# Splitting dt*u*B between the GpSimd and tensor engines by phase, and C of pair 0 on the vector engine in phases 7 and 11

## The reference, cut to what matters

```python
# d = 512 channels, 16 states per channel, 4 sequences (batches) of 512 steps
u = silu(conv1d(in_proj_w @ ctx) + conv_b)
dt_lo, Bm, Cm = split(x_proj_w @ u)              # 16, 16 and 16 rows
delta = softplus(dt_proj_w @ dt_lo + dt_proj_b)
def step(state, xs):                             # state: channels x 16
    dA = exp(d_t[..., None] * A)
    state = state * dA + (d_t * u_t)[..., None] * B_t[:, None, :]
    y_t = einsum('ben,bn->be', state, C_t)
y = (scan of step + D * u) * silu(layernorm(x))
x = x + tanh(g_xattn) * y
x = x + tanh(g_ffn) * ffn(layernorm(x))          # router, top 2 of 32 experts of rank 16
```

## Time and profile before

| | |
|---|---|
| median of 3 runs | 546.57 us |
| the three runs | 546.57, 546.42, 549.73 us |
| time of the profiled execution | 550.42 us |
| its span (first to last instruction) | 548.6 us |
| busy: PE, PEld | 490.2 us (89%), 361.4 us (66%) |
| busy: DVE, ACT, POOL | 481.8 us (88%), 393.8 us (72%), 456.5 us (83%) |
| mean granted PE clock | 0.96 |

### The profile page before, as it was taken

How to read it: one execution, slowest core, us unless ns; L and a number is a source line. 1 busy time by engine, 2 the same in 40 slices (tenths; PEclk the granted TensorE clock), 3 DMA queues, 4 the chain that set the end, 5 groups by cost and what they waited for, 6 DMA issues and landing times.

```text
span 548.6 us, 9113 instructions
## 1 busy us (share of the span) xinstructions
PE 490.2 (89%) x2962; PEld 361.4 (66%) x2962; DVE 481.8 (88%) x884; ACT 393.8 (72%) x704; POOL 456.5 (83%) x337
## 2 busy tenths in 40 slices
PE   6687989898888799999998999998999999899688
PEld 2156979767766486766776776657666666675654
DVE  3868999978989999979999999889899889999852
ACT  3268697847685878586886868595988888888542
POOL 0169999969999998979999999979799899887910
PEclk9656999999989899999999999999999999999799
DMA  5794000107520000047230000068100000000001
GB/s 102 265 340 158 1 2 1 39 7 268 193 76 2 2 1 32 27 154 254 78 97 1 20 2 20 1 192 289 63 1 21 19 22 10 11 20 20 1 21 38
DMA packets 18705, 39.37 MB, mean 72 GB/s; under 512 B 5585, under 2 KB 6353, under 8 KB 18658
## 3 DMA queue, kind: packets, MB, share of 16 engines
q1 hardware_dynamic: 18658, 38.79, 20.9%
HBM read 34.33 MB, written 4.46 MB: 71 GB/s over the span
## 4 chain that ended last, share of the span: by engine, by line
PE 53%; DVE 21%; ACT 13%; issue 9%; POOL 2%; DMA 1%; DVEq 0%; ACTq 0%; SPq 0%; POOLq 0%
PE p_s L744 12%; PE p_y L766 11%; DVE state L1228 10%; PE p_v L799 7%; PE p_f L790 6%; PE p_tr L711 3%; PE p_pr L667 3%; PE p_pr L674 3%; ACT da L985 2%; PE p_pr L686 2%; DVE x L1170 2%; DVE p_s L1228 2%; PE p_f L779 1%; ACT L938 1%; ACT p_s L985 1%
## 5 line engine op out<-in xcount | busy, mean ns | idle before, releaser
L564 POOL TENSOR_TENSOR state<-state,c_bc 128x1024 f32<-128x1024 f32 (+1 forms) x131 | 256.5, 1970 | 21.7 <-DVE state L1228 19.6
L744 PEld LDWEIGHTS p_s<-pair_b,du_t 128*128 128x128 f32 x1072 | 139.4, 198 | 41.9 <-issue 29.7
L744 PE MATMUL p_s<-pair_b,du_t 128*128 128x128 f32 x1072 | 152.8, 285 | 13.6 <-DVE state L1228 10.6
L549 POOL TENSOR_TENSOR dbu<-du,pair_b 128x1024 f32<-128x1024 f32 (+1 forms) x80 | 145.2, 1818 | 5.6 <-DMA pair_b<-bc_rows 4.2
L766 PE MATMUL p_y<-ident,state 128*128 128x128 f32 x1024 | 148.7, 275 | 0.0
L985 ACT ACTIVATE p_s<-delta,a_neg 128x512 f32<-128x512 f32 (+1 forms) x162 | 93.6, 581 | 66.9 <-DVE state L1246 33.5
L1228 DVE TENSOR_TENSOR_SCAN state<-da,p_s 128x512 f32<-128x512 f32 (+1 forms) x116 | 134.5, 1173 | 7.3 <-PE p_s L744 6.7
L766 PEld LDWEIGHTS p_y<-ident,state 128*128 128x128 f32 x1024 | 120.8, 143 | 23.7 <-issue 22.7
L985 ACT ACTIVATE da<-delta,a_neg 128x512 f32<-128x512 f32 (+1 forms) x158 | 100.4, 648 | 15.6 <-DVE state L1228 15.3
L1228 DVE TENSOR_TENSOR_SCAN state<-p_s,dbu 128x512 f32<-128x512 f32 (+1 forms) x100 | 98.3, 998 | 1.9 <-POOL dbu L549 1.8
L790 PE MATMUL p_f<-u_sb,h_t 128*128 128x512 f32 x112 | 56.9, 612 | 1.2 <-DVE gw L1329 1.2
(11 more groups left out here) (180 smaller groups left out, 662.5 us busy)
## 6 DMA issues: line engine op xcount, KB each, us to landing
c_bc<-bc_rows SPq DMA_DIRECT2D x32, 512.0 KB, 5.4
pair_b<-bc_rows SPq DMA_DIRECT2D x16, 512.0 KB, 6.2
xs<-in_x SPq DMA_DIRECT2D x16, 256.0 KB, 4.7
out<-ot SPq DMA_DIRECT2D x14, 256.0 KB, 2.0
cx<-in_ctx_t SPq DMA_DIRECT2D x4, 512.0 KB, 3.5
u_sb<-in_u_w SPq DMA_DIRECT2D x1, 1024.0 KB, 7.3
v_sb<-in_v_w SPq DMA_DIRECT2D x1, 1024.0 KB, 14.7
w_in<-in_in_w_t SPq DMA_DIRECT2D x1, 384.0 KB, 4.7
```

The costliest lines, as they stand in the source:

```text
L549: eng.tensor_tensor(dbu[:, i % 2, :, 0:w], du[:, 0:w].unsqueeze(1).to_broadcast([P, 2, w]), rows_of_b(p)[:, :, c0:c0 + w], ALU.mult).then_ ...
L564: eng.tensor_tensor(pair, pair, c_bc[:, 2 * p:2 * p + 2, c0:c0 + w], ALU.mult).then_inc(po_cs, 1)
L744: mm = eng.matmul(p_s[g % BANKS][:, t * P:(t + 1) * P], du_t[:, f % 2, t, :], diagonals_of(n // 2)[:, n % 2, c0 // P + t, :], start=(t == ...
```

## The change

In phases 3, 7 and 11 one pair more is made by POOL and not by PE: pair 1 in phase 3, pair 2 in phases 7 and 11. Its rows of B are loaded one phase earlier, over the diagonals, by a DMA of its own (`broadcast_b_once`); the place is needed as rows, or rebuilt as diagonals, in the next batch anyway. In phases 7 and 11 DVE takes over C of pair 0 from POOL. In phase 19 pair 6 moves from POOL to PE, with four diagonals made by ACT behind decays 4 to 7 (`diagonals_for_last`), and C of pair 1 moves from DVE to POOL. The places of `times_b` in POOL's list come from a table, `BEHIND_C`, and are the same as before for sets that were there before.

```diff
+ONE_MORE = [1, 2, 2]
+ONE_LESS = 6
+BEHIND_C = {
+    (2, 5): {2: -4, 5: 2},
...
+    (1, 2, 3, 5, 7): {1: -3, 2: -2, 3: 0, 5: 1, 7: 3},
...
-    def pool_pairs(b):
-        return POOL_SETS[b]
+    def pool_pairs(f):
+        b, k, c0, w = PHASE[f]
+        if k == Q - 1 and b + 1 < B:
+            return sorted(POOL_SETS[b] + [ONE_MORE[b]])
+        return [p for p in POOL_SETS[b] if f < LAST or p != ONE_LESS]
...
-    PAIRS_BY_DVE += [(f, p) for f in range(SPLIT, F) for p in (1, 4)]
+    PAIRS_BY_DVE += [(f, p) for f in range(SPLIT, F) for p in (1, 4) if (f, p) != (LAST, 1)]
     PAIRS_BY_DVE += [(f, 1) for f in range(Q - 1, SPLIT)] + [(f, 5) for f in range(Q - 1, SPLIT, Q)]
+    PAIRS_BY_DVE += [(f, 0) for f in range(2 * Q - 1, SPLIT, Q)]
...
+            def broadcast_b_once(f, p):
+
+                eng.wait_ge(pe_dbu, by_pe[f - 1, 2 * p + 1] + 1)
+                broadcast(PHASE[f][0], 2 * p, rows_of_b(p)).then_inc(s_bbc[p], 16)
...
+                if k == Q - 2 and b + 1 < B:
+                    broadcast_b_once(f + 1, ONE_MORE[b])
                 if f >= 6:
                     store_out(f - 6)
...
-                if k == 0 and c0 == 0:
-                    eng.wait_ge(s_bbc[p], 16 * broadcasts_of_b(b, p))
+                if k == 0 and c0 == 0 or p not in pool_pairs(f - 1):
+                    eng.wait_ge(s_bbc[p], 16 * broadcasts_of_b(f, p))
...
+                def behind_c(c):
+                    for p in pool_pairs(f):
+                        if BEHIND_C[tuple(pool_pairs(f))][p] == c:
+                            times_b(f, p)
+                    if f < LAST:
+                        for p in pool_pairs(f + 1):
+                            if BEHIND_C[tuple(pool_pairs(f + 1))][p] == c - PAIRS:
+                                times_b(f + 1, p)
...
+                if f == LAST and n // 2 == ONE_LESS:
+                    eng.wait_ge(ac_diag, 2 * Q * (B - 1) + Q // 2 * (n % 2 + 1))
...
+            def diagonals_for_last(n, t):
+
+                if n == 2 * ONE_LESS and t == Q // 2:
+                    eng.wait_ge(po_dbu, by_pool[LAST - 1, ONE_LESS] + 1)
+                eng.activation(diagonals_of(n // 2)[:, n % 2, t, :], ident[:, :], ACT.Copy,
+                               scale=b_t[:, n, t:t + 1]).then_inc(ac_diag, 1)
...
+                    if f == LAST and n in (4, 5, 6, 7):
+                        diagonals_for_last(2 * ONE_LESS + (n - 4) // 2, Q // 2 + n % 2)
```

More of the change, by code:

```diff
@@ L71, in on_pool @@
     def on_pool(f, n):
-        return n // 2 in POOL_SETS[PHASE[f][0]]
+        return n // 2 in pool_pairs(f)
     def on_dve(f, n):
@@ L79, in flamingo @@
     PE_TILES = [(f, n) for f in range(F) for n in range(NS) if not on_pool(f, n) and not on_dve(f, n)]
-    POOL_TILES = [(f, p) for f in range(F) for p in pool_pairs(PHASE[f][0])]
+    POOL_TILES = [(f, p) for f in range(F) for p in pool_pairs(f)]
     DIAGONALS = [(0, p) for p in pe_pairs(0)[1:] + [0]]
@@ L351, in rows_of_b, with broadcasts_of_b @@
             return pair_b[:, p, :].rearrange("p (n l) -> p n l", n=2)
-        def broadcasts_of_b(b, p):
-            return sum(p in pool_pairs(a) for a in range(b + 1)) + (p == 0)
+        def broadcasts_of_b(f, p):
+            more = [Q * a + Q - 1 for a in range(B - 1) if ONE_MORE[a] == p]
+            return sum(p in POOL_SETS[a] for a in range(PHASE[f][0] + 1)) + sum(a <= f for a in more) + (p == 0)
         ZOPS = 6
@@ L400, in broadcast_b @@
                     before = first_phase(b) - 1
-                    if p in pool_pairs(b - 1):
+                    if p in pool_pairs(before):
                         eng.wait_ge(po_dbu, by_pool[before, p] + 1)
@@ L470, in _ @@
                     broadcast_c(b + 1, 0)
-                    broadcast_b(b + 1, pool_pairs(b + 1)[0])
+                    broadcast_b(b + 1, POOL_SETS[b + 1][0])
                     broadcast_c(b + 1, 1)
-                    broadcast_b(b + 1, pool_pairs(b + 1)[1])
+                    broadcast_b(b + 1, POOL_SETS[b + 1][1])
+                if k == Q - 2 and b + 1 < B:
+                    broadcast_b_once(f + 1, ONE_MORE[b])
                 if f >= 6:
@@ L478, in _ @@
                     broadcast_c(b + 1, 3)
-                    for p in pool_pairs(b + 1)[2:]:
+                    for p in POOL_SETS[b + 1][2:]:
                         broadcast_b(b + 1, p)
@@ L530, in times_u @@
                 eng.wait_ge(pe_turn, TURN["du", f - 1] + 1)
-                eng.wait_ge(po_dbu, by_pool[f, pool_pairs(b)[0]])
+                eng.wait_ge(po_dbu, by_pool[f, pool_pairs(f)[0]])
                 if f == 1:
@@ L546, in times_b @@
                     eng.wait_ge(ve_scan, 2)
-                if p == pool_pairs(b)[0]:
+                if p == pool_pairs(f)[0]:
                     wait_for_du(eng, f)
@@ L598, in _ @@
                 b, k, c0, w = PHASE[f]
-                pairs = pool_pairs(b)
                 turning = k == Q - 1 and b + 1 < B
                 turned = k == 0 and b and c0 == 0
-                many = len(pairs) >= Q
-                five = len(pairs) == 5
-                next_first = f < LAST and (PHASE[f + 1][0] != b or many)
+                early_u = k == 0 and b == 0
+                def behind_c(c):
[6 more added lines that the diff above has]
+                                times_b(f + 1, p)
                 times_c(f, 0)
@@ L607, in _ @@
                     diagonals(0, 0)
-                if five:
-                    times_b(f, pairs[2])
-                elif many or len(pairs) == 3:
-                    times_b(f, pairs[1])
+                behind_c(0)
                 if turned:
@@ L617, in _ @@
                 times_c(f, 1)
-                if many and not five:
-                    times_b(f, pairs[2])
+                behind_c(1)
                 if turned:
@@ L622, in _ @@
                 times_c(f, 2)
-                if five or not many:
-                    times_b(f, pairs[3] if five else pairs[-1])
-                early_u = k == 0 and c0 == 0
-                if early_u and not many:
+                behind_c(2)
+                if early_u:
                     times_u(f + 1)
                 times_c(f, 3)
-                if many:
-                    times_b(f, pairs[-1])
-                if f < LAST and not (early_u and not many):
+                behind_c(3)
+                if f < LAST and not early_u:
                     times_u(f + 1)
                 times_c(f, 4)
-                if f < LAST and PHASE[f + 1][0] == b and not many:
-                    times_b(f + 1, pairs[0])
+                behind_c(4)
                 if turning:
@@ L640, in _ @@
                 times_c(f, 5)
-                if next_first:
-                    times_b(f + 1, pool_pairs(PHASE[f + 1][0])[0])
+                behind_c(5)
                 if k and STATS.get(f):
@@ L648, in _ @@
                 times_c(f, 6)
-                if next_first and len(pool_pairs(PHASE[f + 1][0])) == 5:
-                    times_b(f + 1, pool_pairs(PHASE[f + 1][0])[1])
+                behind_c(6)
                 if turning:
@@ L734, in make_dbu @@
                     eng.wait_ge(ac_turn, TURN["du", f] + 1)
-                if b == 0 and n == 0:
+                if f == LAST and n // 2 == ONE_LESS:
+                    eng.wait_ge(ac_diag, 2 * Q * (B - 1) + Q // 2 * (n % 2 + 1))
+                elif b == 0 and n == 0:
                     eng.wait_ge(po_diag, DIAGONALS.index((0, 0)) + 1)
```

1 line of the change is left out of this document (added), and 4 rows, old and new, of the table BEHIND_C.

## The result

The changed kernel took **553.15 us** (median of 15 runs, 549.04 to 555.61) against 548.49 us (15 runs, 546.2 to 551.68) of the kernel before on the same chip: a ratio of **1.0067**, 95% interval 1.0042 to 1.0092. The ratio is taken over all the runs and is not the quotient of the two medians (that would be 1.0085). By the ratio the kernel is slower by 0.7%, or 3.7 us; by the medians, 4.7 us. The prediction had 1.6 us less. The profiled execution took 554.72 us, with a span of 553.0 us.

The account below looks back on a forecast made before the run. DVE bounds ordinary phases; in turning phases 3, 7 and 11 it waits on a PE-ACT-PE chain. Terms -1.06 - 0.7 - 0.7 + 0 + 0.9 = -1.6 us gave 545.0 us, range 541.8 to 547.9.

Parts of the forecast that it names:

- rival (a): Widened PE gaps before the dt projection of phases 3, 7, 11 halve the clock; all three: +3.5 us, 550.1 us; chance 0.12.
- Phase 3, -1.06: Phase 3: PE loses two tiles, but only tile 2 moves the dt projection up; -1.06 us, from 0 to -2.1.
- Phases 7 and 11, -0.7 each: Phases 7 and 11: tile 5 gives 1.0 us, decay 5's new wait costs 0.3; -0.7 us each, +0.3 to -2.
- the two products on DVE: Phases 7 and 11: DVE's two added C products, 1.3 us, are hidden in its 2.48 us wait for the router scores.
- POOL, 0: Phases 7 and 11: POOL ends about 0.9 us late, regained in the next phase; 0 us, up to +0.6.
- rival (c): POOL bounds behind phases 7 and 11; its lateness eats the 0.7 us gained both times; 546.4 us, chance 0.2.
- The wait that was foreseen in phase 12: Start of phase 12: DVE waits about 0.6 us for POOL's pair 3, regained by scan 9.
- Phase 19, +0.9: Phase 19: PE's eight more records ahead of tile 14, partly at half clock, cost +0.9 us; bounds -1.4 and +1.7.
- The lower bound, -1.4: Phase 19: with PE at full clock all through, the wait of 1.35 us before scan 14 goes; -1.4 us.
- The part of C of pair 1: Phase 19: DVE saves two short products, but scan 6 waits for POOL's pair 3 as already (0.43 us); 0 us.
- (b): Phases 3, 7 and 11: both tiles count, giving 3 x 2.1 = 6.3 us; 540.3 us, chance 0.10.
- (d): No gain arrives, since a later wait takes it back phase by phase; with phase 19's 0.9 us, 547.5 us; chance 0.1.

Follow-up runs that it names:

- Filled: Changed kernel plus twelve idle matmuls (result changes nothing, PE kept issuing) before the dt projection of phases 3, 7 and 11: 546.89 us, ratio 0.9953.
- the kernel before, filled: Kernel before plus idle matmuls in its own PE gaps, in phases 3, 4, 5, 7, 11 and 19: 544.8 us, ratio 0.994.

## Why the prediction was wrong

The step that failed is that the sum has no term for the clock. It took for granted that PE's clock stays at 1.00 in the gaps in front of the dt projection that the change itself makes, on the ground that PE works right before and right behind them, and left the fall to rival (a) with a chance of 0.12. The trace showed gaps of the length forecast (1.66, 1.71 and 1.70 us against "about 1.8") and behind two of them half a clock. Filled, the same kernel went from a ratio of 1.0067 to 0.9953. Rival (a) named the place and the mechanism; it should have been the forecast. Its sum, +3.5 us or a ratio of 1.0064, is close to the measured 1.0067, and that is in part luck: in the trace two gaps of its three had falls, and the rest of the loss came from falls in places that it does not name. The Trainium skill's sentence that the prediction weighed ("TensorE: Matmul & The Clock Gate", Part 1: activity is what lifts the throttle) was read from the wrong side. By that, the trace of the changed kernel agrees too, with a clock of 0.50 behind the gaps of 1.66 and 1.71 us, and the sentence spoke for the rival: the change takes activity away just there.

- **The price of a fall.** Rival (a) took 1.7 us a fall. The runs gave 1.1 and 1.2 us in phase 3 (phases 2 and 3 with 55.14 and 55.22 against 54.02 filled), 1.6 in phase 11 (32.37 against 30.72), 1.6 in phase 7 for one stretch and 3.4 for one twice as long. So 1.7 was about right for a single one. That it can last twice as long was not in the rival's sum.
- **Falls elsewhere.** Neither the forecast nor the rival had falls in phases that the change leaves alone. Phases 5 and 9 lost 1.2 and 1.1 us in the profiled execution, nearly as much together as phase 7, and phases 6 and 11 another 0.2 and 0.3 in their wake. The gaps there are old; where in time they lie has moved.
- **Phase 3, -1.06.** Right in size: -0.94 at full clock, with phase 2. In the changed kernel the fall took more than that back (55.22 against 54.95).
- **Phases 7 and 11, -0.7 each.** Right in size: like against like, each gave -0.61 (32.94 against 33.55, 30.73 against 31.34). The -0.35 of phase 11 in some runs is this less the 0.27 us from a fall in phase 9. That the two products on DVE are hidden under the score wait was right: 1.23 us against the forecast 1.2; filled, 0.86 in phase 7 with them and 2.22 without. (The 2.48 us of the earlier trace rows hold the 0.27 us of the fall in phase 5; the kernel before, filled, waits 2.22.)
- **POOL, 0; rival (c).** Right: with one product more on POOL nothing moved. That C of pair 2 comes one instruction later (242.91 us in phase 7) harmed no scan of phases 7 and 8. The wait that was foreseen in phase 12 came, 0.32 us long at scan 6 against "about 0.6", and was gone again by scan 9, as the prediction had it: the phase has 20.23 us in every run but one, 20.24.
- **Phase 19, +0.9.** Between what the clock makes of it: +0.43 at full clock, +1.1 and +1.71 at half. The lower bound, -1.4 with PE at full clock, mixed two things: the clock alone is worth that (13.86 against 15.29 us), and the two tiles add to it even then. The part of C of pair 1 was right: scan 6 waits 1.40 us for POOL where it waited 0.43, and the two products saved are gone in that.
- **Rivals (b) and (d).** No turning phase gained 2 us, and (d) is out, since with the clock up the gains arrive in the phases.

The sum of the mechanisms, -1.6 us, was thus near what they measure (-1.73), and it was of no use: between two kernels that differ by 1.7 us of work, the clock decides with more. The fills took 0.6% (3 us) off the kernel before and 1.4 to 1.6% (8 to 9 us) off the changed one. What stays open is which gaps have a fall behind them in a given execution. The same instructions had one in phase 11 in one run and none in another, and the gap of phase 9, left unfilled, had one in three filled versions of the change and none in two others or in the kernel before filled. That the falls of 5 and 9 were moved there by the change's own shift of the later phases was not tried apart from it.
